# A graph network on one core: 36 instead of 25 steps of edge records requested in the sorting phase

## The chip, the cores and the metric

The kernel runs on one core of a Trainium2 chip. The time is the device time of one execution in microseconds (us), taken without a profiler; a second execution, with the hardware profiler on, gave the trace. The core has these engines: TensorE (PE, matmuls; PEld is its weight load), VectorE (DVE), ScalarE (ACT), GpSimd (POOL) and SyncE (SP, which here only issues DMAs). Each runs its own list of instructions in order; they meet by semaphores, and at the end of a phase by a barrier of all engines.

## The reference

Four graph layers over 3125 nodes with 32 channels and 100000 edges (`src`, `dst`, a weight each; the edges come sorted by `dst`). After each layer its result is added to the layer's input and normalised over the channels.

```
x = layernorm(x + segment_sum(x[src], dst))            # 1: sum of the neighbours
x = layernorm(x + L1(x))                               # 2: ten times f += max(0, max over edges of (f[dst] - f[src]) * sqrt(w)), by src
x = layernorm(x + L2(x))                               # 3: three gated graph convolutions
x = layernorm(x + L3(x))                               # 4: an MLP of four layers on every edge, mean by dst
```

## The kernel before

The edges are first brought into two orders on the chip. Both sorts are bitonic: 128 x 1024 keys, VectorE does the compare stages (`tensor_tensor` min and max, lines 396 and 397), and fourteen times the square is turned by TensorE (line 380) and copied back by ScalarE (line 386). The key of the first sort is the pair (group of `dst`, `src`), with the number of the edge in its low bits; the second sort is by `dst`.

After the first sort every edge has a slot. There are 232 tiles of 512 slots, taken as 58 steps (`STEPS1`) of 4 tiles, and a step has 16 sub-tiles (`STEP_SUBS`) of 128 slots. What belongs to the slot's edge, its `dst` and its weight (a record of 8 bytes), is fetched by GpSimd, one indirect DMA for each sub-tile: 128 rows of `edges_dram` at the indices in one column of `record_index`, into one column of `got`. That is `gather_records` (lines 306 to 310), 16 requests a step, 928 in all.

**The sorting phase** (lines 511 to 865) ends in one barrier. VectorE: histogram 0, fill keys, sort 0, `record_index` (line 776), slot tables, sort 1, `slots_by_dst`, histogram 1 (lines 667 to 685), a few small tables. Histogram 1 has 40 steps (`EF // EB`); in each VectorE writes `one_low` (line 675), `one_high` (line 678) and three products with the parts of the weights (lines 680 to 683), all `tensor_tensor` with two inputs in SBUF, and TensorE adds them up by 20 matmuls (line 600). There are two buffers, so step n waits until TensorE is through with step n - 2 (`hot_used`, line 672). GpSimd, once line 777 has told it that the indices are there, runs lines 581 to 583: all requests of the first `STEPS_FIRST` steps, then a wait until they have landed. The barrier behind it needs GpSimd as well as VectorE.

**The first layer's phase** (lines 1046 to 1265) requests the other steps:

```
for k in range(STEPS_FIRST, STEPS1):          # GpSimd, lines 1061 to 1066
    if k >= STEPS_FIRST + 4:
        pool.wait_ge(got_in[k % 4], records_of(k - 4))
    gather_records(pool, k, got_in[k % 4])
```

Beside it VectorE makes, for each of the 58 steps, one `source_made` tile (line 1235, 128 x 2048) and then 16 one-hot tiles `dst_hots_first` and `dst_kept` (line 1249, 128 x 640) out of `dst_col`, which is taken from `got` (line 1226): at one stroke for the steps of the sorting phase, and step by step for the others, after a wait for that step's records (line 1238). TensorE finds the rows (line 1148), ScalarE copies them (line 1200), and TensorE sums them with the one-hots (lines 1160 and 1161). Line 1251, behind the loop, reads the weights out of `got`.

Later phases (the second layer's tile loop, the gates, the MLP layer with its 719 gathers at line 914) have the same code before and after.

Of the kernel before, what the change touches and what calls it, by code (L numbers as in the profile page):

```python
# [114 lines left out]
def program(nc, x, src, dst, edge_weight, conv_w, conv_b, wc, bg, W1, b1, W2, b2, W3, b3, W4, b4, out):  # L115
# [55 lines left out]
    with ctx:  # L171
# [129 lines left out]
        group_base = sb("group_base", [P, SUBTILES], F32, records)  # L301
        got = sb("got", [P, SUBTILES, 2], I32, records)

        STEPS_FIRST = 25

        def gather_records(pool, k, got_in):

            for n in range(k * STEP_SUBS, (k + 1) * STEP_SUBS):
                pool.indirect_dma_start(got[:, n, :], None, edges_dram,  # L309
                                        bass.IndirectOffsetOnAxis(ap=record_index[:, n:n + 1], axis=0)).then_inc(got_in, 16)  # L310
# [35 lines left out]
        with ExitStack() as own:  # L346
# [164 lines left out]
            with phase("sort_in0", "turn_ready0", "turned_done0", "copied0", "keys_out0", "sort_in1", "turn_ready1", "turned_done1", "copied1", "keys_out1",  # L511
# [51 lines left out]
                def _(pool):  # L563
# [16 lines left out]
                    pool.wait_ge(edge_ready, 1)  # L580
                    for k in range(STEPS_FIRST):
                        gather_records(pool, k, got_done)
                    pool.wait_ge(got_done, 16 * STEPS_FIRST * STEP_SUBS)

# [438 lines left out]
        with ExitStack() as own:  # L1023
# [22 lines left out]
            with phase("vec", "norm_ready", "norm_root", "const_done", "ident_ready", "got_in0", "got_in1", "got_in2", "got_in3", "src_in0", "src_in1", "source_ready",  # L1046
# [8 lines left out]
                def records_of(k):  # L1055
                    return 16 * STEP_SUBS * len(range(STEPS_FIRST + (k - STEPS_FIRST) % 4, k + 1, 4))

                @block.gpsimd
                def _(pool):
                    pool.iota(node_row[:, :], [[1, DST_NODES]], base=0, channel_multiplier=0).then_inc(const_done, 1)  # L1060
                    for k in range(STEPS_FIRST, STEPS1):
                        if k >= STEPS_FIRST + 4:
                            pool.wait_ge(got_in[k % 4], records_of(k - 4))
# [152 lines left out]
                def _(dve):  # L1216
# [8 lines left out]
                    def columns_of(some):  # L1225
                        link(V.scalar_tensor_tensor(dst_col[:, some], got[:, some, 0], 1.0, group_base[:, some], ALU.mult, ALU.subtract))

                    columns_of(slice(0, STEPS_FIRST * STEP_SUBS))
                    for k in range(STEPS1 + 1):
# [950 lines left out]
```

## Time and profile before

| | us |
|---|---|
| three executions without the profiler | 8461.82, 8480.76, 8480.96 (median 8480.76) |
| span of the profiled execution | 9642.0 |
| VectorE, TensorE, GpSimd busy in that span | 6437.2, 6289.8, 3063.5 |
| GpSimd's 928 record requests, busy | 940.6 |

The profiled span is 1161 us longer than the median. The result names no time around the span for the profiled execution, so the span itself stands for it.

Times in rows of the trace are in us from the span's start. A row of a timeline gives the start, the duration, the engine, the line, the operation, what it writes and reads, and in brackets the idle time of its engine before it with what released it. "remote" is a semaphore of another engine, "issue" that the profile shows nothing that was waited for. A request of GpSimd is shown from its start to the end of its work on GpSimd, not to the landing of the data.

### The profile page before, as it was taken

Reading aid. Unit: us, or ns where it says so; the run is one execution under the profiler, and the core shown is the slowest. Engines: PE = TensorE matmul, PEld = TensorE weight load, DVE = VectorE, ACT = ScalarE, POOL = GpSimd, SP = SyncE. Lnnn points to the kernel's source line nnn. Section 1 sums busy time; section 2 is a strip of 40 time slices with the busy share of each in tenths; the row PEclk is TensorE's granted clock in tenths of the full one; section 3 lists DMA queues with packets and bytes.
Section 4 is the critical chain, followed back from the end, with each engine's and each line's share of the span. In section 5 each row is a group of like instructions: output and inputs, shape, how many; then the busy total and the mean of one; then the engine's idle time right before and its main releaser. Section 6 shows DMA issues by size and latency. Waiting matters only on the chain. (4 is left out here: it accounts for less than half of the span.)

```text
span 9642.0 us, 139065 instructions
## 1 busy us (share of the span) xinstructions
PE 6289.8 (65%) x41922; PEld 3109.5 (32%) x41922; DVE 6437.2 (67%) x10345; ACT 3431.3 (36%) x4321; POOL 3063.5 (32%) x2943
## 2 busy tenths in 40 slices
PE   3100120028787979888898879788798989365555
PEld 2100120013443434334343434343344545222222
DVE  8864560017687878787787878787888989433333
ACT  0000000002255545555555555455444444132333
POOL 0047527740032323332232323332300000555553
PEclk9999985559899989999999989899899999677777
DMA  2000001128666667666676666566576767111110
GB/s 83 3 13 1 5 22 25 17 76 294 218 229 202 227 196 238 204 215 218 204 241 200 226 205 235 198 213 213 185 273 232 291 231 290 32 22 22 22 22 24
DMA packets 480504, 1461.81 MB, mean 152 GB/s; under 512 B 109553, under 2 KB 145049, under 8 KB 412582
## 3 DMA queue, kind: packets, MB, share of 16 engines
q1 hardware_dynamic: 228800, 1119.91, 33.6%
q10 hardware_dynamic: 157440, 298.89, 8.7%
q0 software_dynamic: 93568, 33.84, 3.0%
q8 instruction: 423, 6.93, 0.3%
q14 instruction: 273, 2.24, 0.1%
HBM read 1160.35 MB, written 292.22 MB: 151 GB/s over the span
## 5 line engine op out<-in xcount | busy, mean ns | idle before, releaser
L1435 PE MATMUL acc<-dst_hot,parts 128*128 128x512 bf16 x11600 | 3024.8, 387 | 575.1 <-issue 355.7
L1494 ACT ACTIVATE parts_out<-acc 96x1024 bf16<-96x1024 f32 x2320 | 2343.1, 1020 | 2018.0 <-PE acc L1446 1751.2
L1398 POOL DMA_INDIRECT group_best<-best_dram,best_row x1250 | 1361.0, 1089 | 3012.0 <-SPq L1361 2615.7
L1310 DVE TENSOR_SCALAR dst_hot<-dst_rows,node_f 128x2048 bf16<-128x2048 int16 x2910 | 2051.8, 740 | 180.1 <-PE acc L1446 138.7
L1435 PEld LDWEIGHTS acc<-dst_hot,parts 128*128 x11600 | 1057.6, 98 | 1868.2 <-issue 768.6
L914 POOL DMA_INDIRECT gathered<-table_dram,source_index x719 | 731.7, 1018 | 1800.2 <-POOLq L158 1300.5
L309 POOL DMA_INDIRECT got<-edges_dram,record_index x928 | 940.6, 1014 | 860.7 <-DVEq L777 548.8
L1446 PE MATMUL acc<-source,parts 128*128 128x128 bf16 x9280 | 922.6, 223 | 9.8 <-DMA source<-source_dram 4.5
L1446 PEld LDWEIGHTS acc<-source,parts 128*128 x9280 | 640.7, 99 | 642.7 <-issue 361.8
L1517 DVE SCALAR_TENSOR_TENSOR risen<-rise,factor 128x512 f32<-128x512 f32 x580 | 401.1, 692 | 588.0 <-PE rise L1458 322.3
L1523 DVE TENSOR_TENSOR_SCAN best<-joined,best,risen 128x512 f32<-128x512 uint8 x570 | 728.6, 1278 | 0.7
L1249 DVE TENSOR_SCALAR dst_hots_first<-node_row,dst_col 128x640 bf16<-128x640 int16 x464 | 179.0, 386 | 793.6 <-remote 456.2
L1768 ACT ACTIVATE found<-rows_found 128x384 bf16<-128x384 f32 x696 | 341.7, 491 | 618.0 <-PE rows_found L1705 614.9
L1723 PE MATMUL sums_by_dst<-dst_hots,edge_message 128*96 128x512 bf16 x1392 | 547.0, 393 | 16.0 <-DVE dst_hots L1798 2.1
L1723 PE MATMUL sums_by_dst<-dst_kept_in,edge_message 128*96 128x512 bf16 x1392 | 553.9, 398 | 0.9
L2121 DVE SCALAR_TENSOR_TENSOR value<-starts,ps 128x256 f32<-128x256 f32 (+1 forms) x110 | 43.9, 399 | 745.5 <-DMA best_dram<-zero_rows 662.5
L1148 PE MATMUL rows_found_first<-parts,source_made 128*128 x928 | 83.4, 216 | 670.0 <-issue 597.8
L1798 DVE TENSOR_SCALAR dst_hots<-node_row,dst_col 128x640 bf16<-128x640 int16 x1392 | 486.5, 382 | 30.3
L1200 ACT ACTIVATE found_first<-rows_found_first 128x384 bf16<-128x384 f32 x232 | 113.9, 491 | 1066.8 <-remote 686.7
L380 PE MATMUL turned<-identity,ping 128*128 128x128 f32 x224 | 55.1, 427 | 660.0 <-issue 360.2
L600 PE MATMUL hist<-one_high,one_low 125*128 125x125 bf16 (+1 forms) x1600 | 166.3, 297 | 399.6 <-DVEq L684 371.3
L1532 DVE STREAM_TRANSPOSE best_out<-best 128x512 f32<-128x512 f32 x580 | 408.1, 704 | 2.1
(376 smaller groups left out, 8013.5 us busy)
## 6 DMA issues: line engine op xcount, KB each, us to landing
dst_rows<-step_dst_dram SPq DMA_DIRECT2D x291, 1024.0 KB, 4.2
source<-source_dram SPq DMA_DIRECT2D x291, 1024.0 KB, 6.7
dst_kept_in<-dst_hot_dram SPq DMA_DIRECT2D x174, 1280.0 KB, 5.6
best_dram<-best_out ACTq DMA_DIRECT2D x580, 256.0 KB
factor<-step_weight_dram ACTq DMA_DIRECT2D x560, 256.0 KB
sources<-source_dram SPq DMA_DIRECT2D x174, 512.0 KB, 6.6
dst_hot_dram<-dst_kept SPq DMA_DIRECT2D x58, 1280.0 KB
src_rows<-step_src_dram SPq DMA_DIRECT2D x58, 512.0 KB
```

The source lines that it names most:

```text
L309: pool.indirect_dma_start(got[:, n, :], None, edges_dram, bass.IndirectOffsetOnAxis(ap=record_index[:, n:n + 1], axis=0)).then_inc(got_in, 16)
L914: pool.indirect_dma_start(gathered[k % 2][:, t, :], None, table_dram, bass.IndirectOffsetOnAxis(ap=source_index[:, at:at + 1], axis=0)).th ...
L1310: nc.vector.tensor_scalar(hot[k % 2][b][:, :], index_rows[k // 2 % 2][:, k % 2, :], node_f[:, b:b + 1], None, ALU.is_equal).then_inc(hot_r ...
L1398: pool.indirect_dma_start(group_best[:, g, h, :], None, best_dram, bass.IndirectOffsetOnAxis(ap=best_row[:, i:i + 1], axis=0)).then_inc(en ...
L1435: nc.tensor.matmul(acc[n % 3][:, 0:TILE], blocks[b], hot[k % 2][b][:, q * TILE:(q + 1) * TILE], start=(b == 0), stop=(b == DST_BLOCKS - 1))
L1446: last = nc.tensor.matmul(acc[n % 3][:, TILE + j * P:TILE + (j + 1) * P], blocks[DST_BLOCKS + j], source[k // 2 % 2][:, k % 2, at:at + P], ...
L1494: act.activation(moved[n % (2 * QUADS)][:, :], acc[n % 3][0:SPLIT, :], ACT.Copy).then_inc(tile_moved, 1)
L1517: V.scalar_tensor_tensor(risen[:, :], rise[c % 2][:, :], 0.0, factor[c % 3][:, :], ALU.max, ALU.mult).then_inc(risen_ready, 1)
L1523: V.tensor_tensor_scan(best[c % 2][:, :], joined[:, c, :], risen[:, :], best[(c - 1) % 2][:, TILE - 1:TILE] if c else 0.0, ALU.mult, ALU.m ...
L1532: V.transpose(best_out[c % 3][:, :], best[c % 2][:, :]).then_inc(turned_ready, 1)
L1723: nc.tensor.matmul(to[0], message[c % 2][:, i, :], one_hot[:, 0:BANK], start=False, stop=False)
L1798: V.tensor_scalar(dst_hot[n % HOTS2][:, :], node_row[:, :], dst_col[:, s:s + 1], None, ALU.is_equal).then_inc(hot_ready, 1)
```

## The change

One number: how many steps' records are requested in the sorting phase. Nothing else is touched; `records_of`, the slice of line 1228 and the test in line 1237 follow from it.

```
--- before.py
+++ after.py
@@ -301,7 +301,7 @@
-        STEPS_FIRST = 25
+        STEPS_FIRST = 36
```

On GpSimd, in the order of its instructions, the sorting phase ends with the first run of requests (line 309, `got<-edges_dram,record_index`; line 158 belongs to the barrier), and `node_row` begins the first layer's phase:

```order
 L578 AFFINE_SELECT upto<-ones 128x128
-L309 DMA got<-edges_dram,record_index 128x2 x400
+L309 DMA got<-edges_dram,record_index 128x2 x576
 L151 UNCONDITIONAL_BRANCH
 L158 ISA
 L1058 UNCONDITIONAL_BRANCH
 L1060 IOTA node_row 128x640
-L309 DMA got<-edges_dram,record_index 128x2 x528
+L309 DMA got<-edges_dram,record_index 128x2 x352
```

176 requests, 11 steps of 16, stand ahead of the barrier instead of behind it.

On VectorE, at the start of the first layer's phase, the first `dst_col` covers the records that are there:

```order
 L1220 CAST identity_first<-identity 128x128
 L1222 CAST sum_f<-sum_parts 96x32
-L1226 SCALAR_TENSOR_TENSOR dst_col<-got,group_base 128x400
+L1226 SCALAR_TENSOR_TENSOR dst_col<-got,group_base 128x576
 L1235 TENSOR_SCALAR source_made<-src_rows,node_f 128x2048 x2
 L1249 TENSOR_SCALAR dst_hots_first<-node_row,dst_col 128x640
```

The later single columns of line 1226, each with its wait for one step's records, begin at step 36 instead of 25: eleven of them are gone.

## Rows read from the trace of the kernel before

**Rows 1.** The page's rows of the requests and of the MLP layer's gathers.

```profile
L914 POOL DMA_INDIRECT gathered<-table_dram,source_index x719 | 731.7, 1018 | 1800.2 <-POOLq L158 1300.5
L309 POOL DMA_INDIRECT got<-edges_dram,record_index x928 | 940.6, 1014 | 860.7 <-DVEq L777 548.8
```

**Rows 2.** GpSimd's timeline, from histogram 1's start into the next phase.

```profile
1096.75 2.42 POOL L309 DMA_INDIRECT got<-edges_dram,record_index  x1 [0.30 <-issue]
...
1103.47 3.46 POOL L309 DMA_INDIRECT got<-edges_dram,record_index  x1 [0.30 <-issue]
1107.23 1.00 POOL L309 DMA_INDIRECT got<-edges_dram,record_index  x1 [0.30 <-issue]
...
1127.47 0.94 POOL L309 DMA_INDIRECT got<-edges_dram,record_index  x1 [0.30 <-issue]
1376.10 0.68 POOL L1060 IOTA node_row<- 128x640 int16 x1 [247.69 <-DMA got<-edges_dram,record_index]
1377.09 0.95 POOL L309 DMA_INDIRECT got<-edges_dram,record_index  x1 [0.30 <-issue]
```

**Rows 3.** VectorE's timeline in histogram 1: its first steps, one later, the last.

```profile
1095.49 2.86 DVE L675 TENSOR_TENSOR one_low<-low,ramp 125x2560 bf16<-125x2560 bf16 x1 [2.43 <-remote]
...
1103.28 2.83 DVE L675 TENSOR_TENSOR one_low<-low,ramp 125x2560 bf16<-125x2560 bf16 x1 [2.19 <-issue]
...
1134.00 2.83 DVE L675 TENSOR_TENSOR one_low<-low,ramp 125x2560 bf16<-125x2560 bf16 x1 [25.16 <-remote]
...
1155.19 2.83 DVE L675 TENSOR_TENSOR one_low<-low,ramp 125x2560 bf16<-125x2560 bf16 x1
...
1160.89 2.83 DVE L675 TENSOR_TENSOR one_low<-low,ramp 125x2560 bf16<-125x2560 bf16 x1
...
1358.18 2.11 DVE L682 TENSOR_TENSOR one_high<-one_high,w_parts 125x500 bf16<-125x500 bf16 x3
```

**Rows 4.** VectorE: start and end of sort 0, start and end of sort 1.

```profile
301.79 0.43 DVE L403 TENSOR_SCALAR ping<-ping 128x512 f32<-128x512 f32 x1
...
569.27 0.69 DVE L397 TENSOR_TENSOR ping<-ping 128x512 f32<-128x512 f32 x1
...
628.03 0.43 DVE L403 TENSOR_SCALAR ping<-ping 128x512 f32<-128x512 f32 x1
...
1054.11 0.69 DVE L397 TENSOR_TENSOR ping<-ping 128x512 f32<-128x512 f32 x1
```

**Rows 5.** GpSimd alone by stretch: us, busy (x requests), PEclk, DMA share, GB/s.

```profile
589.00:628.00 39.00, 30.29 (x29) 1.00 0.18 39
628.00:724.00 96.00, 74.05 (x73) 1.00 0.04 1
...
1055.00:1095.00 40.00, 30.85 (x31) 1.00 0.11 24
```

**Rows 6.** The first layer's loop: two requested steps, the last request, two free steps, the end.

```profile
1519.37 0.75 DVE L1235 TENSOR_SCALAR source_made<-src_rows,node_f 128x2048 bf16<-128x2048 int16 x1
1653.77 0.75 DVE L1235 TENSOR_SCALAR source_made<-src_rows,node_f 128x2048 bf16<-128x2048 int16 x1
...
2089.12 0.94 POOL L309 DMA_INDIRECT got<-edges_dram,record_index  x1 [0.30 <-issue]
...
2120.01 0.75 DVE L1235 TENSOR_SCALAR source_made<-src_rows,node_f 128x2048 bf16<-128x2048 int16 x1
...
2545.53 0.63 DVE L1251 COPY w_col<-got 128x928 f32<-128x928 f32 x1
```

**Rows 7.** The chain of waits, two successive chunks of the MLP layer.

```profile
8925.42 2.24 DVE at_starts L988
...
8984.14 2.19 DVE at_starts L988
```

**Rows 8.** The trace's list of waits, second layer's loop, waits for other engines' semaphores.

```profile
DVE risen L1517 <- remote: 229.1, 62, 8.2
...
ACT parts_out L1494 <- remote: 192.6, 55, 10.6
```

## The prediction

> **What bounds the kernel now.** I read first the page's groups of GpSimd instructions, because only its requests move: 928 of them, 940.6 us busy [rows 1]. Then GpSimd's timeline around the barrier: the last of the 400 requests of the sorting phase begins at 1127.47, and GpSimd stands idle for 247.69 us until 1376.10 [rows 2]. That gap is what the change wants to fill: 11 steps are 176 requests, and at 0.95 + 0.30 = 1.25 us each, the pace of an undisturbed one, they are 220 us. The row names the landing of `got` as the releaser, but the last request was over 247 us before; what ended the phase was VectorE with histogram 1, whose last products begin at 1358.18 [rows 3].
>
> Then the first layer's phase. Its 528 requests run from 1377.09 to 2090.06: 713 us, 1.350 us each. VectorE's loop reaches its end only at 2545.53, and the reader should see how oddly it gets there: while requests go on, a step takes 1653.77 - 1519.37 = 134.4 us; once they have ended, the loop goes from 2120.01 to 2545.53 through 51 sets of one-hots, 8.34 us each [rows 6]. So in the trace the requests do not merely feed the loop, they hold it up. The same shows in sort 1, which takes 1054.80 - 628.03 = 426.8 us beside requests where sort 0, the same instructions, takes 268.2 us without them [rows 4]; and in histogram 1, where the third step begins 30.7 us after the second, after 25.16 us of waiting for another engine's semaphore, while an undisturbed step takes 5.70 [rows 3].
>
> **Does the untraced execution have these late signals?** On this the sum hangs, since the span is 9642.0 us and the median 8480.76: 1161 us go away with the profiler. I work out what would go if no signal were late and requests kept their pace. Sorting phase: sort 1 gets 268 us long, so histogram 1 starts at 628 + 268 + 41 (what lies between sort 1's end and it) = 937, takes 40 x 5.70 = 228 us, and the 16 us from its last product to the next phase follow: 1181 instead of 1376, 195 us less [rows 2 to 4]. First layer's loop: bound by requests, 528 x 1.315 (the pace beside a busy VectorE, 96 us for 73 [rows 5]) = 694, and 11 for the last landing and step: 705 us instead of 1169, 464 less. MLP layer: a chunk takes 58.7 us [rows 7] and has 719 / 22 = 32.7 gathers [rows 1]; at 1.315 they are 43.0 us, 22 x 15.7 = 345 less. Together 1004. Up to some 230 us more may lie in the second layer's loop, whose waits for late semaphores sum to 229.1 and 192.6 us on two engines, partly at the same time [rows 8]. 1004 to 1234 holds the 1161 that is missing. So I take it that untraced the signals are on time and that requests cost what they cost here, and make the sum for that execution, with the trace's durations.
>
> **The sum.** Removed and added: no instruction but eleven `dst_col` columns on VectorE, which is nothing in a loop of 484 us. 176 requests move across one barrier.
>
> How many requests fit beside the sorting phase's other work? From the start at 589 to sort 1: 29; sort 1: 268 / 1.315 = 204; up to histogram 1: 31 [rows 5]. Beside histogram 1 a row decides. `one_low` takes 2.83 of a step's 5.70 us [rows 3], and the requests that meet it take 2.42 and 3.46 us instead of 0.95: the second starts at 1103.47, `one_low` ends at 1106.11, and the request ends at 1106.93, 0.82 after it [rows 2, 3]. Behind the other four, 0.7 us long, a request waits for 0.05 to 0.2 us. So a request gets through only between two of VectorE's instructions; at a pace of 1.25 it gets one at the end of `one_low`, one 1.4 us later, one at the step's end, and the fourth meets the next `one_low`: three a step, 120 in 40 steps. Behind the histogram 10 more: 394 in all. The Trainium skill ("SBUF - State Buffer", Who interferes with whom) says that a VectorE instruction with two inputs in SBUF contends with a GpSimd instruction that reads SBUF; it also says that a `tensor_tensor` was not seen to stall a DMA. An indirect request reads its indices from SBUF, and by the 3.46 us the trace agrees with the first sentence; by the second the sum would be that of the first rival below.
>
> So before, 400 requests end 6 x 1.25 = 8 us behind VectorE: without late signals, GpSimd's requests already go on beside the whole second histogram, and the gap of 247.69 us is not there. After, 576 - 394 = 182 are left when VectorE is done, and go out with every other engine waiting at the barrier: 182 x 1.25 = 228 us. The sorting phase gets 220 us longer.
>
> The loop gets shorter: 705 us before; after, 352 requests need 463 us and VectorE's 58 x 8.34 + 4 = 488 us, so VectorE becomes the bound: 217 us saved. Cover that goes: the requests of steps 36 to 57 stay ahead of VectorE by 25 us at the end, and if the pace were 1.40 they would bound again (493). Nothing new is queued behind a wait: the wait for `got_done` stands at the phase's end as before.
>
> 220 - 217 = +3 us: 8481 + 3 = 8484. What is unknown is the pace beside the loop, which the trace does not show with VectorE at full speed. Lower end 1.25 (undisturbed): 671 - 488 = 183 saved, +37. Upper end 1.350 (the loop's own rows): 724 - 488 = 236 saved, -16. I take 1.315, the pace measured beside a busy VectorE. The forecast's own range is 8465 to 8518.
>
> **Rivals.**
>
> First, requests go through beside the histogram at 1.25 us. For it: four and three requests start in the first two steps, and only two steps were seen beside requests [rows 2, 3]. Against it: the 3.46 us. Then 228 / 1.25 = 182 fit there, 456 in all; before has slack, after is left with 120, 150 us: 150 - 217 = -67, 8414.
>
> Second, the signals are late without the profiler too. For it: the trace, as it stands. Against it: the 1161 us, which nothing else in the trace explains. Then at 1095 some 199 of the 576 are left, 249 us; beside them the histogram gets on by a step in 30.7 us (10 steps done, 30 left: 171 us, and 21 until the signals are on time again: 1536 instead of 1360, +176) or in half of that (18 done: +130). The loop loses 11 x 16 x 1.35 = 238 us of held-up time, in which 1.8 steps of 8.34 were done: -223. In all -47 to -93, about 8410 if the same stands untraced.
>
> Third, on the other side: requests are cheaper without the profiler, 1.0 us, because part of the 0.30 us behind each belongs to its recording. For it: the 0.30 is the same behind nearly every request [rows 2], whatever VectorE does. Against it: the loop would be bound by 528 x 1.05 + 11 = 565 us and an MLP chunk by 34.4, and with the 195 the trace would shed 195 + 604 + 535 = 1334 us, more than the 1161. Then 39 + 214 + 40 + 120 + 13 = 426 fit, before has slack, after is left with 150, 150 us longer; the loop saves 565 - 488 = 77: +73, 8554. It decides from the point where the loop before is less than 220 us above VectorE's 488.
>
> That the change does not do what it says is part of the forecast: in it the eleven steps go out behind the second histogram, not beside it.
>
> **How the numbers follow.** Forecast 0.50, first rival 0.14, second 0.13, third 0.23. About 0.3%, 25 us, is what a measurement tells from no change. Of the forecast's 0.50 some 0.38 lie within 25 us, 0.06 on either side. Faster: 0.14 + 0.13 + 0.06 = 0.33; same 0.38; slower 0.23 + 0.06 = 0.29. The range runs from just under the first two rivals to the third: 8400 to 8560.
>
> **What would show it.** The profiled execution of the changed kernel will have late signals as this one does, so its span is no measure of the median; by the second rival's sum it should be some 50 to 90 us shorter than 9642. In it: 576 requests ahead of `node_row`; GpSimd's idle time before `node_row` down from 247.69 us, and histogram 1 with steps far longer than 5.70 us until the 576th; requests of 2.4 to 3.5 us there wherever `one_low` runs; in the loop about 475 us of requests, steps of 134 us in it and 8.3 behind it. If requests beside the histogram stay near 1.25 us with VectorE busy, the first rival is right. The forecast is wrong by its central step if the median falls by over 60 us, which needs slack in the sorting phase that I do not find, or rises by over 60, which needs a cheaper request.

## The result, and the profile after

| | us |
|---|---|
| kernel before, 8 executions | 8477.08 (8456.72 to 8481.32) |
| changed kernel, 8 executions | 8494.01 (8484.21 to 8518.56) |
| ratio, with its 95% interval | 1.0027 (1.0015 to 1.0039) |

The change costs 0.27%, between 0.15 and 0.39%: some 13 to 33 us; the medians differ by 17. That is little, but beyond the scatter: the fastest of the eight executions with 36 steps (8484.21) is slower than the slowest of the eight before (8481.32). The forecast was 8484, +3 on the kernel before.

The trace of the changed kernel has a span of 8490.0 us, in line with its untraced times, and none of the late signals that [rows 3] and [rows 6] show. Those were the property of one long profiled execution, not of the kernel: a second trace of the kernel before, taken with the experiments, has a span of 8483.4 us and none either. It is the one that the changed kernel is set beside from here on.

The barrier first. The changed kernel's GpSimd timeline (start and duration in us; in brackets the idle time before the instruction and what ended it), where [rows 2] had an idle time of 247.69 us before `node_row`:

```profile
1417.85 0.94 POOL L309 DMA_INDIRECT got<-edges_dram,record_index  x1 [0.30 <-issue]
1423.05 0.68 POOL L1060 IOTA node_row<- 128x640 int16 x1 [4.26 <-DMA got<-edges_dram,record_index]
1423.88 0.95 POOL L309 DMA_INDIRECT got<-edges_dram,record_index  x1 [0.15 <-issue]
```

VectorE's timeline at the same place:

```profile
1423.21 0.48 DVE L1219 MEMSET identity_first<- 128x512 uint32 x1 [262.18 <-PEq L158]
```

GpSimd no longer waits, but for 4.26 us between the last request's end and `node_row`, its landing among them; VectorE now stands at the barrier for 262.18 us. The page's group of all requests, in the changed kernel and then in the second trace of the kernel before:

```profile
L309 POOL DMA_INDIRECT got<-edges_dram,record_index x928 | 988.7, 1065 | 845.8 <-DVEq L777 549.2
```

```profile
L309 POOL DMA_INDIRECT got<-edges_dram,record_index x928 | 989.1, 1066 | 840.1 <-DVEq L777 548.9
```

All requests together take as long as before (988.7 us busy against 989.1); it is the others that wait for them.

Histogram 1 of the changed kernel, GpSimd's timeline and then VectorE's:

```profile
944.22 2.67 POOL L309 DMA_INDIRECT got<-edges_dram,record_index  x1 [0.30 <-issue]
947.19 1.00 POOL L309 DMA_INDIRECT got<-edges_dram,record_index  x1 [0.30 <-issue]
948.49 1.13 POOL L309 DMA_INDIRECT got<-edges_dram,record_index  x1 [0.30 <-issue]
949.92 2.66 POOL L309 DMA_INDIRECT got<-edges_dram,record_index  x1 [0.31 <-issue]
```

```profile
943.24 2.83 DVE L675 TENSOR_TENSOR one_low<-low,ramp 125x2560 bf16<-125x2560 bf16 x1
945.98 0.67 DVE L678 TENSOR_TENSOR one_high<-high,ramp 125x500 bf16<-125x500 bf16 x1
946.69 2.11 DVE L682 TENSOR_TENSOR one_high<-one_high,w_parts 125x500 bf16<-125x500 bf16 x3
948.94 2.83 DVE L675 TENSOR_TENSOR one_low<-low,ramp 125x2560 bf16<-125x2560 bf16 x1
```

Three requests in 5.70 us, step after step: one that started during `one_low` and ends at 946.89, 0.82 us after it (946.07), and two between the short instructions. VectorE's steps keep their 5.70 us, as long as a step without requests in [rows 3]: only GpSimd pays.

### The profile page after: what moved, and what is told of

It reads as the page before. It is cut to its first block and busy times, and to the rows that moved or that the text cites. A ratio compares the mean times of both kernels' runs of the same rounds, so it can differ in the third digit from the quotient of the medians.

```text
span 8490.0 us, 139043 instructions
## 1 busy us (share of the span) xinstructions
PE 6088.7 (72%) x41922; PEld 3052.1 (36%) x41922; DVE 6446.6 (76%) x10334; ACT 3457.5 (41%) x4321; POOL 3253.6 (38%) x2943
## 5 line engine op out<-in xcount | busy, mean ns | idle before, releaser
L1435 PE MATMUL acc<-dst_hot,parts 128*128 128x512 bf16 x11600 | 2935.1, 382 | 332.4 <-issue 325.3
L1494 ACT ACTIVATE parts_out<-acc 96x1024 bf16<-96x1024 f32 x2320 | 2367.1, 1020 | 1720.3 <-PE acc L1446 1703.3
L1398 POOL DMA_INDIRECT group_best<-best_dram,best_row x1250 | 1411.0, 1129 | 2687.3 <-SPq L1361 2295.9
L914 POOL DMA_INDIRECT gathered<-table_dram,source_index x719 | 823.8, 1146 | 1522.5 <-POOLq L158 1303.8
L309 POOL DMA_INDIRECT got<-edges_dram,record_index x928 | 988.7, 1065 | 845.8 <-DVEq L777 549.2
L1962 PE MATMUL ps<-identity,message 128*128 128x128 f32 x418 | 84.8, 336 | 378.4 <-DVEq L2112 290.3
L386 ACT ACTIVATE ping<-turned 128x1024 f32<-128x1024 f32 x28 | 28.7, 1024 | 784.8 <-PE turned L380 784.8
L1724 PE MATMUL sums_by_dst<-dst_hots,edge_message 128*96 128x128 bf16 x1392 | 306.1, 220 | 0.0
```

What stands on the lines that cost most here:

```text
L309: pool.indirect_dma_start(got[:, n, :], None, edges_dram, bass.IndirectOffsetOnAxis(ap=record_index[:, n:n + 1], axis=0)).then_inc(got_in, 16)
L914: pool.indirect_dma_start(gathered[k % 2][:, t, :], None, table_dram, bass.IndirectOffsetOnAxis(ap=source_index[:, at:at + 1], axis=0)).th ...
L1398: pool.indirect_dma_start(group_best[:, g, h, :], None, best_dram, bass.IndirectOffsetOnAxis(ap=best_row[:, i:i + 1], axis=0)).then_inc(en ...
L1435: nc.tensor.matmul(acc[n % 3][:, 0:TILE], blocks[b], hot[k % 2][b][:, q * TILE:(q + 1) * TILE], start=(b == 0), stop=(b == DST_BLOCKS - 1))
L1494: act.activation(moved[n % (2 * QUADS)][:, :], acc[n % 3][0:SPLIT, :], ACT.Copy).then_inc(tile_moved, 1)
```

## The experiments

The theory (A): the kernel is bound by GpSimd's requests from 589 us to the end of the first layer's loop, on both sides of the barrier, wherever the requests stand; beside histogram 1 only three pass in a step; and from some 35 steps on the loop has fewer requests than VectorE has work, so that each further step is a loss. The rivals stand with the runs.

**The kernel before once more.** No edit.

> The kernel before once more, for a trace without late signals to set beside the trace of the changed kernel. Theory A (requests bound the sorting phase and the loop before, and get through three to a step beside histogram 1): the requests go on to about 1194 us, GpSimd's idle time before node_row is 5 us, not 248; histogram 1 has steps of 5.70 us with requests of 1.00, 1.13 and 2.66 us; the loop from node_row to line 1251 takes about 694 us (528 requests at 1.295 and 10). Theory B (the gap of 248 us is real, and the changed kernel loses by something else): the requests end near the start of histogram 1 and GpSimd idles for over 100 us.

Measured: 8485.09 us (one execution). First the engines by stretch, in the trace of this run: before histogram 1, beside it, behind it, in the loop. Then GpSimd's timeline at the barrier, and VectorE's at the barrier and at the loop's end; of the runs that follow, the passing of the barrier and the loop's end are shown:

```profile
589.00:920.50 331.50, 27.93 (x113) 22.07 (x113) 259.10 (x413) 15.62 (x15) 251.03 (x246) 1.00 0.06 8
920.50:1148.50 228.00, 72.40 (x785) 63.91 (x786) 218.01 (x200) 0.00 (x0) 188.80 (x119) 1.00 0.03 1
1165.00:1195.00 30.00, 0.00 (x0) 0.00 (x0) 0.00 (x0) 0.00 (x0) 21.34 (x23) 1.00 0.04 1
1201.00:1878.00 677.00, 414.18 (x2777) 220.06 (x2777) 347.66 (x1006) 113.94 (x232) 515.56 (x529) 0.83 0.63 208
```

```profile
1192.10 0.95 POOL L309 DMA_INDIRECT got<-edges_dram,record_index  x1 [0.30 <-issue]
1200.51 0.68 POOL L1060 IOTA node_row<- 128x640 int16 x1 [7.46 <-DMA got<-edges_dram,record_index]
```

```profile
1200.66 0.48 DVE L1219 MEMSET identity_first<- 128x512 uint32 x1 [39.84 <-PEq L158]
...
1884.76 0.64 DVE L1251 COPY w_col<-got 128x928 f32<-128x928 f32 x1
```

The columns of the first fence are busy us and instructions (x) of TensorE, its weight load, VectorE, ScalarE and GpSimd, then TensorE's granted clock as a share of full speed, the DMA engines' busy share and GB/s. 246 requests before the histogram, 119 beside it (40 x 3 = 120), and the last 23 go out while every other engine has nothing to do. The requests end at 1193.05, 32 us behind VectorE's work (1200.66 - 39.84 = 1160.82): with 25 steps the sorting phase is already bound by them, and they already go on beside the whole second histogram. The gap of [rows 2] is not there. Theory B falls.

**30 steps.**

```
-        STEPS_FIRST = 25
+        STEPS_FIRST = 30
```

> 30 steps in the sorting phase. Theory A: both phases stay bound by requests, so 80 requests only change their place, at 1.28 us each on either side of the barrier: no change to the kernel before, within 10 us (8477, 8467 to 8487); GpSimd's requests in the sorting phase end near 1297 us. Rival C (every step moved costs the same, 17 us / 11 = 1.5 us): +8 us, 8485, which alone is not told from A.

Measured: 8482.87 us against 8488.71 for the kernel before on the same chip, ratio 0.9992 (0.9981 to 1.0002). No change. The barrier moves from 1200.5 to 1300.4 us, the end of the loop from 1884.8 to 1882.5:

```profile
1300.42 0.68 POOL L1060 IOTA node_row<- 128x640 int16 x1 [4.88 <-DMA got<-edges_dram,record_index]
```

```profile
1882.46 0.63 DVE L1251 COPY w_col<-got 128x928 f32<-128x928 f32 x1
```

100 us are added to one phase and 102 taken from the next. Rival C's +8 us lies outside the interval, which ends at +2; the next run sets the two further apart.

**40 steps.**

```
-        STEPS_FIRST = 25
+        STEPS_FIRST = 40
```

> 40 steps in the sorting phase. Theory A: the loop behind the barrier is bound by VectorE (about 475 us) from some 35 steps on, so each further step only lengthens the sorting phase by 16 x 1.28 = 20.5 us: 4 x 20.5 = 82 us over the changed kernel, about 8576, 99 over the kernel before (ratio 1.0117). Rival C (1.5 us for every step moved): +23 us over the kernel before, 8500.

Measured: 8573.69 us, ratio 1.0101 (1.0086 to 1.0117), 85 us over the kernel before, where 99 were expected. The barrier stands at 1507.4, the loop's end at 1983.0: 475.6 us of loop as with 36 steps (474.9), and 84 us more in front of it. Rival C expected +23 and falls. The reader can see where the bound changes from VectorE's list of waits for the records of a step, from the loop's start to its end, of the kernels with 20, 25 and 30 steps:

```profile
DVE dst_col L1226 <- DMA got<-edges_dram,record_index: 364.1, 26, 15.0
```

```profile
DVE dst_col L1226 <- DMA got<-edges_dram,record_index: 243.4, 18, 15.0
```

```profile
DVE dst_col L1226 <- DMA got<-edges_dram,record_index: 123.6, 10, 14.6
```

It falls by 120 us for every five steps, and with 36 and with 40 steps the row is gone. On that line it would be at zero near 35. What bounds the loop from there on is not VectorE alone. With 36 steps, VectorE's and TensorE's waits in the loop are:

```profile
DVE dst_hots_first L1249 <- PE sums_first L1161: 68.0, 145, 1.5
DVE source_made L1235 <- DMA src_rows<-step_src_dram: 43.8, 32, 5.3
```

```profile
PE sums_first L1160 <- DVE dst_kept L1249: 39.7, 56, 1.4
PE sums_first L1160 <- DVE dst_hots_first L1249: 22.5, 38, 1.3
```

VectorE waits for TensorE's sums and for the source rows, 112 of 475 us, and TensorE for VectorE's one-hots. Which of them a faster kernel would have to shorten was not tried.

**36 steps, the long instruction in four pieces.** `one_low` of histogram 1 is written by four instructions of a quarter of its columns, with the same values.

```
-    V.tensor_tensor(one_low[0:EP, n % 2, :, :], low16[0:EP, part]..., ramp16..., ALU.is_equal)
+    PIECE = EB // (4 if o else 1)
+    for a in range(0, EB, PIECE):
+        V.tensor_tensor(one_low[0:EP, n % 2, a:a + PIECE, :], low16[0:EP, s * EB + a:s * EB + a + PIECE]..., ramp16..., ALU.is_equal)
```

> 36 steps, and the 2.83 us one_low instruction of histogram 1 is written as four of a quarter of its columns; the same values. Theory A (a request passes only between two VectorE instructions that read two inputs from SBUF): no request of 2.66 us is left, four pass in a step instead of three, 40 more in 40 steps, and the sorting phase ends 40 x 1.28 = 51 us earlier less what the splitting costs VectorE (under 10 us): about 8445, ratio to the kernel before 0.996. Rival D (requests are slow beside any busy VectorE, whatever the length of its instructions): still three a step, 8494 to 8504.

Measured: 8447.67 us, ratio to the kernel before 0.9952 (0.9938 to 0.9966). VectorE and GpSimd beside histogram 1, and the same stretches as above (the histogram is now 8 us longer):

```profile
932.18 3.03 DVE L677 TENSOR_TENSOR one_low<-low,ramp 125x640 bf16<-125x640 bf16 x4
...
938.09 3.03 DVE L677 TENSOR_TENSOR one_low<-low,ramp 125x640 bf16<-125x640 bf16 x4
```

```profile
932.45 1.37 POOL L309 DMA_INDIRECT got<-edges_dram,record_index  x1 [0.30 <-issue]
934.13 1.17 POOL L309 DMA_INDIRECT got<-edges_dram,record_index  x1 [0.30 <-issue]
935.60 1.02 POOL L309 DMA_INDIRECT got<-edges_dram,record_index  x1 [0.30 <-issue]
936.92 1.13 POOL L309 DMA_INDIRECT got<-edges_dram,record_index  x1 [0.30 <-issue]
938.36 1.38 POOL L309 DMA_INDIRECT got<-edges_dram,record_index  x1 [0.30 <-issue]
```

```profile
589.00:920.00 331.00, 27.92 (x113) 22.05 (x113) 258.73 (x412) 15.62 (x15) 250.33 (x246) 1.00 0.06 8
920.00:1150.00 230.00, 70.23 (x760) 61.94 (x760) 220.65 (x313) 0.00 (x0) 180.29 (x155) 1.00 0.04 1
```

```profile
1381.98 0.68 POOL L1062 IOTA node_row<- 128x640 int16 x1 [4.27 <-DMA got<-edges_dram,record_index]
```

```profile
1855.29 0.64 DVE L1253 COPY w_col<-got 128x928 f32<-128x928 f32 x1
```

Four requests a step, none over 1.38 us, 155 in the stretch where 119 passed with 25 steps and 120 with 36, though VectorE is as busy as before. The barrier comes 41.1 us earlier than in the changed kernel and the loop's end 42.7. What held the requests up was the length of one VectorE instruction; rival D falls.

**20 steps.**

```
-        STEPS_FIRST = 25
+        STEPS_FIRST = 20
```

> 20 steps in the sorting phase: the other side. Theory A: 320 requests are done before VectorE, which then ends the sorting phase near 1170 us instead of 1200 (25 steps); the loop is bound by 608 requests at 1.282 (684 us for 528 with 25 steps) and gets 787 us long: +72 us over the kernel before, ratio 1.0085, and GpSimd idles for some 50 us before node_row. Rival E (it is the sum of all requests that bounds the kernel, wherever they stand): no change, ratio 1.000.

Measured: 8543.68 us against 8481.88 for the kernel before, ratio 1.0078 (1.0063 to 1.0093). Here, of the kernels without the split, is the gap that the first trace seemed to show with 25 steps:

```profile
1164.76 0.68 POOL L1060 IOTA node_row<- 128x640 int16 x1 [103.25 <-DMA got<-edges_dram,record_index]
```

```profile
1947.30 0.64 DVE L1251 COPY w_col<-got 128x928 f32<-128x928 f32 x1
```

The gap is 103 us, twice the 50 that was expected; the last of the 320 requests starts at 1058.85, still beside the histogram. The sorting phase ends with VectorE, 36 us earlier than with 25 steps, and the loop is 98 us longer. Rival E falls: the sum of the requests bounds only while neither phase has slack.

**25 steps with the split.** The split alone; `STEPS_FIRST` stays at 25, as in the kernel before.

> 25 steps with the one_low instruction in four pieces. Theory A: 246 requests before histogram 1 and 155 beside it are the 400, so they end with VectorE, and the sorting phase ends near 1175 us instead of 1200; the loop stays 684 us: 25 us less than the kernel before (ratio 0.997), 5 to 15 us more than the split with 36 steps. If splitting helped in some other way than by letting requests through, the gain would be the 42 us of the 36 steps again.

Measured: 8449.9 us, ratio 0.9965 (0.9952 to 0.9978).

```profile
1171.67 0.68 POOL L1062 IOTA node_row<- 128x640 int16 x1 [21.63 <-DMA got<-edges_dram,record_index]
```

```profile
1853.85 0.64 DVE L1253 COPY w_col<-got 128x928 f32<-128x928 f32 x1
```

The requests have some 12 to 17 us of slack now (21.63 less the 4 to 10 us that stand there where they end last); VectorE ends the phase 29 us earlier than the requests did with 25 steps, and that is all that can be had there. Against the kernel before, the gain is 0.35%, and that of the split with 36 steps 0.48%: 11 us apart, where 5 to 15 had been expected, but the intervals overlap, and in the traces the loop's end comes 1.4 us earlier with 25. Which of the two is faster is not told.

**30 steps with the split.** The two edits above, with `STEPS_FIRST = 30`.

> 30 steps with the one_low instruction in four pieces, meant as the best of both: requests are never the thing that waits, neither at the barrier nor behind VectorE in the loop. Theory A: 79 requests are left when histogram 1 ends, the sorting phase ends near 1265 us, the loop takes 582 us as with 30 steps before: 38 us less than the kernel before (ratio 0.9955), 5 to 10 us less than the split with 36 steps.

Measured: 8429.99 us, ratio 0.9942 (0.9929 to 0.9955), the lowest of all, though the interval overlaps those of the other two splits.

```profile
1259.07 0.68 POOL L1062 IOTA node_row<- 128x640 int16 x1 [4.84 <-DMA got<-edges_dram,record_index]
```

```profile
1839.50 0.64 DVE L1253 COPY w_col<-got 128x928 f32<-128x928 f32 x1
```

The barrier comes 41 us earlier than with 30 steps without the split (1300.4), the loop is as long (580.4 against 582.0), and its end comes 43 us earlier. As was meant, the requests never wait; VectorE waits for them, at the barrier and in the loop:

```profile
DVE identity_first L1221 <- PEq L158: 90.5, 1, 90.5
DVE dst_col L1228 <- DMA got<-edges_dram,record_index: 120.9, 9, 15.0
```

Its loop ends 14 us before that of 25 steps with the split, which leaves requests idle before the barrier, and 16 before that of 36, which has too few of them in the loop to hold it up. With 30 they bound both phases, so no time of GpSimd goes unused in either.

All of it in one table, from the traces:

| steps | barrier passed (us) | loop (us) | loop's end (us) |
|---|---|---|---|
| 20 | 1164.8 | 782.5 | 1947.3 |
| 25 (before) | 1200.5 | 684.3 | 1884.8 |
| 30 | 1300.4 | 582.0 | 1882.5 |
| 36 (changed) | 1423.1 | 474.9 | 1898.0 |
| 40 | 1507.4 | 475.6 | 1983.0 |
| 25, split | 1171.7 | 682.2 | 1853.9 |
| 30, split | 1259.1 | 580.4 | 1839.5 |
| 36, split | 1382.0 | 473.3 | 1855.3 |

## Why the prediction was right, and where not

**The late signals.** The prediction took them for something that the timed execution does not have, from the 1161 us between span and median. That was right, and the sum hung on it. By phases the account was less good, and its errors partly cancel: set beside the second trace, the late one is 176 us longer up to the barrier (195 forecast), 485 in the loop (464), 266 in the second layer's loop (up to 230) and 226 in the MLP layer (345, from 1.315 us a gather; there the second trace has one in 1.46). The prediction then said that the changed kernel's profiled execution would show them again, with steps of 134 us and a span 50 to 90 us below 9642. It does not. What made them in that one execution was not tried and stays open.

**Where the requests stand.** "The gap of 247.69 us is not there", and the requests of 25 steps end 8 us behind VectorE: they end 32 us behind it. Three a step were foreseen, and 119 and 120 were counted beside 40 steps. What was off lies ahead of the histogram: of the 41 us that the sum puts between sort 1's end and histogram 1, taken from the late trace, the second trace has 22.4, and 246 requests fit where 264 were counted. VectorE's timeline there:

```profile
897.09 0.69 DVE L397 TENSOR_TENSOR ping<-ping 128x512 f32<-128x512 f32 x1
...
920.16 2.83 DVE L675 TENSOR_TENSOR one_low<-low,ramp 125x2560 bf16<-125x2560 bf16 x1
```

Before and after the error is the same, so it drops out of the difference; had it gone the other way by more than the 8 us, the kernel before would have had slack and the sum would not hold. That the margin was 32 us and not 8 was not foreseen. That the request waits for the end of the VectorE instruction is shown by the split, which only puts four short instructions in the place of a long one. By the Trainium skill ("SBUF - State Buffer", Who interferes with whom) a VectorE instruction with two SBUF inputs contends with a GpSimd instruction that reads SBUF; the traces agree, with 2.66 us against 0.95. That a `tensor_tensor` was not seen to stall a DMA, which it says as well, does not hold for these indirect requests.

**The sum.** The sorting phase got 222.5 us longer (220 forecast, 176 x 1.25). Where GpSimd works alone in the changed kernel, a request takes 255 / 199 = 1.28 us, since two of them come 3 us late:

```profile
1165.00:1420.00 255.00, 0.00 (x0) 0.00 (x0) 0.00 (x0) 0.00 (x0) 187.67 (x199) 1.00 0.04 1
```

The loop got 209.4 us shorter, where 217 were forecast, and this is the term that was mis-sized: the loop before took 684 us, not 705, since a request beside the loop costs 1.28 us and not the 1.315 taken from beside the sort. The loop after took 475, not 488. That the requests no longer bound it was foreseen; that VectorE alone does is not borne out, it waits for 112 us there. 222.5 - 209.4 = +13 us where +3 was written. 176 requests at 1.28 are 225 us on either side of the barrier, but the loop saves only 209, since it meets its other bound near 35 steps. The measured interval is 13 to 33. No more can be read out of it: behind the loop, where the code is the same, the traces without late signals take between 6576 and 6609 us, and executions of one kernel lie up to 42 us apart (30 steps).

**The rivals.** The first (requests at 1.25 us beside the histogram) is excluded by 2.66 us in every step. The second (late signals untraced) falls with the second trace. The third (cheaper requests) falls with 1.25 us at full quiet in traces as long as the timed runs.

**The words of the change.** The 11 steps do not go on beside the second histogram; 35 of the 400 requests (400 - 246 - 119) were left over behind it before the first of them was added.

## What to carry to other kernels

When a queue of requests bounds two phases, moving requests over the barrier between them gains nothing; look for the slack first, and see in which phase the engine that feeds really idles. What gains is to let the requests through: cut a long VectorE instruction into pieces, if it is the one that they wait behind. And where a profiled span is far above the timed runs, take the waits in it as suspect; the durations of single VectorE and GpSimd instructions were usable here.

## What the runs showed of the hardware that was not expected

One profiled execution of the same kernel was 1159 us longer than another (9642.0 against 8483.4). The excess lies in the phases in which GpSimd issues indirect requests, as set out above; the stretch up to the first request (589 us) and the gates, which have none (1257 us), are as long in both. The long trace's list of waits has rows with "remote" as releaser, up to 686.7 us on one line; the other's has none. VectorE's and GpSimd's instructions took the same in both (5.70 us for a step of the histogram, 0.95 us for a request), TensorE's not everywhere: the median matmul of line 1973, in the MLP layer, took 417 ns in the long one and 631 in the other.

A 128-row indirect request that meets a VectorE `tensor_tensor` with two inputs in SBUF waits for its end and then needs 0.82 us, whether that instruction is 2.83 us long (end at 946.07, the request's at 946.89) or 0.7 (948.80 and 949.62). The VectorE instruction loses nothing: `one_low` took 2.82 to 2.83 us in all 80 steps of the two histograms, and the first has no requests beside it. Four pieces cost VectorE 0.2 us a step (5.91 against 5.70) and let a fourth request through.
